# The output projection of a cross-attention tile, moved behind the first two groups of transposes of the next tile

## The chip, the cores and the metric

One core of a Trainium2 chip runs the whole program: four transformer layers, each a cross-attention and a mixture of experts. The metric is the device time of one launch in microseconds. Engine names are those of the profile: PE (TensorE matmuls), PEld (its weight loads), DVE (VectorE), ACT (ScalarE), POOL (GpSimd), SP (SyncE).

## The reference, cut to what matters

The change touches three of the four cross-attentions: those of layers 0, 2 and 3 (L0, L2, L3). Each adds to the residual `x` (4 batches of 512 tokens, width 128) an attention over 77 context rows:

```python
qh = heads(layernorm(x) @ Wq + bq);  kh = heads(ctx @ Wk + bk);  vh = heads(ctx @ Wv + bv)
score = einsum('bhqd,bhkd->bhqk', qh, kh) / sqrt(D)      # L2: + mask * -1e9, L3: barred keys at -inf
attn = softmax(score, axis=-1)
out = einsum('bhqk,bhkd->bhqd', attn, vh)
x = x + merge_heads(out) @ Wo + bo
```

L0 and L2 have 16 heads of 8, L3 has 8 heads of 64 and no biases. The cross-attention of layer 1 is another function and is not touched.

## The kernel before

`cross_attention` cuts the 2048 tokens into 16 tiles of 128. Every engine has its own program, written out by hand as a Python loop over tiles; within an engine the instructions run in the order in which they are written, and semaphores tie the engines together.

For a tile n, PE's function `tile(n)` does this:

- `turn(n, g)`: four transposes of the probabilities of one group of four heads into a PSUM bank (line 529). It waits for `normed`, which POOL's `divide` (line 441) raises twice for a tile, once for each half of the heads. L0 and L2 have four groups, L3 two.
- ACT's `group_turned` (line 635) copies each turned group to `probT`.
- `product(n, g)`: probabilities by values (line 540 in L0 and L2, 542 in L3). It waits for that copy.
- `scores(n + 3)`: queries by keys for the tile three ahead (lines 95 to 97 in L0 and L2, where each product is split in three; line 518 in L3). In L0 and L2 it stands ahead of the products of groups 2 and 3, in L3 behind all products. It waits until DVE has read the scores of the tile before it.
- ACT's `mixed(n)` (line 639) copies the summed products from PSUM to `mixedT`.
- `output(n)` (line 550): `mixedT` by the output weights, one product in L0 and L2, four in L3. It waits for `mixed(n)` and stands at the end of the tile. DVE's `add(n)` (line 745) adds its result to the residual.
- In tiles 0, 4 and 8 `next_queries` (line 483) also projects the queries of the next batch; ACT copies them (lines 621 and 627). In L0 and L2 that projection goes to the same PSUM bank as the products.

DVE's tile n: `shift(n + 2)` (a maximum over the scores, line 728, and a subtraction, line 729; for unmasked scores of L2 and for L3 first an addition of the mask), `add(n - 1)`, `add_up(n + 1)` (sums and reciprocals of both halves, lines 737 and 738). In tiles 0, 3 and 6 it also lays out the keys of a further batch (`spread_keys`, line 688). ACT's tile n has, between copies, the exponential of tile n + 2 (line 631). Behind the last tile PE transposes two batches for the next stage (`nxt.norm.turn`, line 284), which ACT copies (line 291); then all engines meet at a barrier.

Of the kernel before, what the change touches and what calls it, by code (L numbers as in the profile page):

```python
# [27 lines left out]
TILES = BATCH * SEQ // P  # L28
# [288 lines left out]
def cross_attention(c, norm, fetch, nxt, tag, H, D, score_scale, mask):  # L317
# [26 lines left out]
    with ExitStack() as ctx:  # L344
# [51 lines left out]
        def later(n, k):  # L396
            return 0 <= n + k < TILES

        with nc.Block() as block:
# [68 lines left out]
            def _(pe):  # L468
# [10 lines left out]
                def queries(b, j):  # L479

                    if j >= 2:
                        pe.wait_ge(q_ready, b * FB + j - 1)
                    pe.matmul(ps[:, Q[j % 2], :], wq[:, j * P:(j + 1) * P], c.normT[:, b * SEQ:(b + 1) * SEQ], start=True, stop=True).then_inc(q_done, 1)

                def wait_scores_read(n):
                    if mask is None or masked_on_pe(n):
                        pe.wait_ge(shifted, n + 1)
                    else:
                        pe.wait_ge(masked, masks_added(n) + 1)
# [32 lines left out]
                def turn(n, g):  # L522

                    pe.wait_ge(normed, n * 2 + g * 2 // GROUPS + 1)
                    if g >= 2:
                        pe.wait_ge(turn_read, n * GROUPS + g - 1)
                    for a in range(GROUP):
                        h = g * GROUP + a
                        last = pe.transpose(ps[0:KEYS, TURN + g % 2, a * P:(a + 1) * P], prob[:, n % PROBS, h * KEYS:(h + 1) * KEYS], c.ident[:])  # L529
                    last.then_inc(turned, 1)  # L530

                def product(n, g):

                    if n == 0 and g == 0 and biased:
                        pe.wait_ge(v_ready, GROUP)
                    pe.wait_ge(turn_read, n * GROUPS + g + 1)
                    for a in range(GROUP):
                        h = g * GROUP + a
                        if FB == 1:
                            last = pe.matmul(ps[a * COLS:(a + 1) * COLS, PV, 0:P], v_all[:, n // TPB, h, :], probT[:, h, :], start=(g == 0), stop=(g == GROUPS - 1))  # L540
                        else:
                            last = pe.matmul(ps[h % 2 * D:(h % 2 + 1) * D, PV, h // 2 * P:(h // 2 + 1) * P], v_all[:, n // TPB, h, :], probT[:, h, :], start=True, stop=True)
                    if g == GROUPS - 1:
                        last.then_inc(pv_done, 1)

                def output(n):
                    pe.wait_ge(mixed_ready, n + 1)
                    pe.wait_ge(y_added, n + 1)
                    for j in range(FB):
                        last = pe.matmul(ps[:, Y, 0:P], mixedT[:, j * P:(j + 1) * P], wo[:, j, :], start=(j == 0), stop=(j == FB - 1))  # L550
                    last.then_inc(y_done, 1)

                def tile(n):
                    project = list(range(FB)) if n % TPB == 0 and later(n, TPB) else []

                    def next_queries():
                        if project:
                            queries(n // TPB + 1, project.pop(0))

                    next_queries()  # L560
                    turn(n, 0)
                    next_queries()
                    turn(n, 1)
                    next_queries()
                    for g in range(GROUPS):
                        if g > 0 and g + 1 < GROUPS:
                            turn(n, g + 1)
                        if g == SCORES_AT and later(n, AHEAD):
                            scores(n + AHEAD)
                        product(n, g)  # L570
                        next_queries()
                    if SCORES_AT == GROUPS and later(n, AHEAD):
                        scores(n + AHEAD)
                    output(n)

                if not biased:
                    pe.wait_ge(v_ready, BATCH)
# [15 lines left out]
                for n in range(TILES):  # L593
                    tile(n)
                wait_scores_read(TILES - 1)
                nxt.norm.turn(pe, 0, 0)
                nxt.norm.turn(pe, 1, 1)

            @block.scalar
# [1944 lines left out]
```

## Time and profile before

| | us |
|---|---|
| median of 3 runs | 1961.55 |
| lowest and highest run | 1961.02, 1966.17 |
| span of the profiled execution | 1960.8 |
| tiles of L0, L2 and L3 in it (first product to the barrier) | about 102, 109 and 83 |
| PE busy, share of the span | 93% |
| mean granted TensorE clock | 0.974 |

The span runs from the first to the last instruction. No time of its own is listed for the profiled execution; its span is 0.2 below the fastest run and 0.75 below the median.

### The profile page before, as it was taken

What the parts mean: (1) busy time and instruction counts of PE and PEld (TensorE: products, weight loads), DVE (VectorE), ACT (ScalarE), POOL (GpSimd) and SP (SyncE); (2) the same over time, 40 slices, a digit from 0 to 9 for tenths busy, and PEclk for the clock granted to TensorE, in tenths of its full rate; (3) what the DMA queues carried; (4) which work ended last, traced back from release to release, by engine and by line L of the source; (5) the groups of instructions that cost most, each with busy time, mean ns of one, the idle gap of its engine ahead of it and who ended that gap; (6) DMA issues with size and microseconds to landing.
All of it is one profiled execution on the core that took longest, in us unless ns stands there. A gap on an engine that the chain in (4) does not pass through costs nothing. (4 is left out here: it accounts for less than half of the span.)

```text
span 1960.8 us, 29985 instructions
## 1 busy us (share of the span) xinstructions
PE 1818.4 (93%) x11163; PEld 1272.5 (65%) x11163; DVE 1500.0 (77%) x2712; ACT 1015.9 (52%) x1506; POOL 829.8 (42%) x667
## 2 busy tenths in 40 slices
PE   5888999789999999999989999889899999989898
PEld 4667888544544444445447777677567789967676
DVE  6878986766777676767758888888699965567798
ACT  3656888356666766666644555455400130045686
POOL 3633221266767676767661344365301402012231
PEclk9999999789999999999998999999999999999899
DMA  1001111100000000000000212000000110000032
GB/s 66 2 12 58 65 65 54 52 1 1 1 1 1 1 1 1 1 1 1 1 4 17 87 65 86 13 1 2 17 11 27 32 54 1 0 13 1 22 115 97
DMA packets 21195, 51.52 MB, mean 26 GB/s; under 512 B 3563, under 2 KB 11383, under 8 KB 18116
## 3 DMA queue, kind: packets, MB, share of 16 engines
q1 hardware_dynamic: 20596, 49.53, 7.4%
q8 instruction: 83, 1.36, 0.3%
q14 instruction: 52, 0.43, 0.1%
q10 hardware_dynamic: 464, 0.20, 0.1%
HBM read 48.48 MB, written 1.25 MB: 25 GB/s over the span
## 5 line engine op out<-in xcount | busy, mean ns | idle before, releaser
L1605 POOL TENSOR_TENSOR sb_L_total<-sb_L_total,sb_L_probT 128x512 f32<-128x512 f32 (+1 forms) x192 | 268.7, 1424 | 59.5 <-ACT sb_L_probT L1911 56.6
L441 POOL TENSOR_TENSOR sb_L_prob<-sb_L_prob,sb_L_rsum 128x616 f32<-128x616 f32 (+1 forms) x96 | 105.7, 1123 | 239.6 <-DVE sb_L_rsum L738 239.6
L1911 ACT ACTIVATE sb_L_probT<-banks 128x1024 f32<-128x1024 f32 x128 | 131.3, 1025 | 113.4 <-PE banks L1738 113.2
L1968 DVE TENSOR_REDUCE sb_L_top_tok<-banks 128x2 f32<-128x1024 f32 x128 | 155.7, 1217 | 6.1 <-PE banks L1705 4.3
L1748 PE MATMUL banks<-sb_L_probT,sb_L_v 128*64 128x512 f32 x512 | 137.1, 615 | 0.2 <-DVE sb_L_mixedT L2019 0.2
L2335 DVE SCALAR_TENSOR_TENSOR sb_L2f_hid<-banks,sb_L2f_weight,sb_L2f_hid 128x512 f32<-128x512 f32 x176 | 123.2, 748 | 2.6 <-PE banks L97 1.6
L1602 POOL TENSOR_TENSOR sb_L_total<-sb_L_probT 128x512 f32<-128x512 f32 x64 | 80.7, 1282 | 104.5 <-ACT sb_L_probT L1911 104.5
L2405 DVE SCALAR_TENSOR_TENSOR sb_resid<-banks,sb_L2f_weight,sb_resid 128x128 f32<-128x128 f32 x192 | 67.2, 351 | 60.9 <-PE banks L97 56.3
L1310 DVE TENSOR_TENSOR sb_L0f_hid_low<-sb_L0f_raw,sb_L0f_hid_high 128x1024 fp32r<-128x1024 f32 x64 | 88.3, 1396 | 28.8 <-ACT sb_L0f_hid_high L1266 28.4
L635 ACT ACTIVATE sb_L_probT<-banks 77x512 f32<-77x512 f32 x160 | 86.7, 586 | 41.5 <-PE banks L529 41.5
L1247 ACT ACTIVATE sb_L1f_gate<-banks 112x512 f32<-112x512 f32 x96 | 57.6, 600 | 93.2 <-PE banks L97 93.2
L1986 DVE TENSOR_TENSOR sb_L_q_sq_low<-sb_L_q_sq,sb_L_q_sq_high 128x512 fp32r<-128x512 f32 x32 | 25.4, 793 | 102.1 <-ACT sb_L_q_sq_high L1863 102.1
L1255 ACT ACTIVATE sb_L0f_raw<-banks,sb_L0f_b 128x512 f32<-128x512 f32 x128 | 86.6, 681 | 26.2 <-PE banks L97 26.0
L529 PE MATMUL banks<-sb_ident,sb_L_prob 128*77 128x128 f32 x640 | 92.9, 279 | 0.0
L1303 DVE TENSOR_TENSOR sb_L1f_raw<-sb_L1f_gate,banks 112x512 f32<-112x512 f32 x96 | 65.8, 686 | 35.4 <-PE banks L97 31.9
L263 ACT ACTIVATE sb_norm_root<-sb_norm_square 128x8 f32<-128x8 f32 (+4 forms) x16 | 3.4, 210 | 171.6 <-DVE sb_norm_square L257 147.6
L95 PE MATMUL banks<-sb_L2f_w_high,sb_L2f_hidT_low 128*128 128x384 f32 x256 | 85.6, 334 | 1.7 <-DVEq L2397 1.7
L97 PE MATMUL banks<-sb_L2f_w_high,sb_L2f_hidT_high 128*128 128x384 f32 x256 | 85.5, 334 | 0.0
L96 PE MATMUL banks<-sb_L2f_w_low,sb_L2f_hidT_high 128*128 128x384 f32 x256 | 85.5, 334 | 0.0
L95 PE MATMUL banks<-sb_L2f_w_high,sb_norm_low 128*128 128x512 f32 x192 | 80.8, 421 | 5.0 <-DVE sb_L2f_hid L2335 4.9
L1310 DVE TENSOR_TENSOR sb_L1f_hid_low<-sb_L1f_raw,sb_L1f_hid_high 112x512 fp32r<-112x512 f32 x96 | 85.0, 886 | 0.1
L529 PEld LDWEIGHTS banks<-sb_ident,sb_L_prob 128*77 128x77 f32 x640 | 72.1, 147 | 19.7 <-issue 18.9
(432 smaller groups left out, 5410.4 us busy)
## 6 DMA issues: line engine op xcount, KB each, us to landing
sb_L0f_wide<-spread_L0f SPq DMA_DIRECT2D x7, 1024.0 KB, 6.7
sb_L1f_wide<-spread_L1f SPq DMA_DIRECT2D x7, 1024.0 KB, 7.2
sb_L3f_wide<-spread_L3f SPq DMA_DIRECT2D x7, 1024.0 KB, 4.9
sb_fetched<-L2f_w SPq DMA_DIRECT2D x12, 256.0 KB, 2.6
sb_fetched<-L1f_gu SPq DMA_DIRECT2D x8, 336.0 KB, 3.1
sb_fetched<-L0f_w SPq DMA_DIRECT2D x8, 259.0 KB, 2.9
sb_fetched<-L0f_w SPq DMA_DIRECT2D x8, 256.0 KB, 3.1
sb_normT<-L2f_w SPq DMA_DIRECT2D x2, 768.0 KB, 4.2
```

Of the source, the lines that this page charges most:

```text
L95: pe.matmul(out, sl, mh, start=start, stop=False)
L96: pe.matmul(out, sh, ml, start=False, stop=False)
L441: pool.tensor_tensor(grid, grid, bcast(rsum[:, n % PROBS, half], [None, KEYS]), ALU.mult).then_inc(normed, 1)
L529: last = pe.transpose(ps[0:KEYS, TURN + g % 2, a * P:(a + 1) * P], prob[:, n % PROBS, h * KEYS:(h + 1) * KEYS], c.ident[:])
L635: act.activation(probT[:, g * GROUP:(g + 1) * GROUP, :].rearrange("k h t -> k (h t)"), ps[0:KEYS, TURN + g % 2, :], ACT.Copy).then_inc(tur ...
L1255: act.activation(raw[:, s % lag, f, :], ps[:, n % HBANKS, :], func, bias=bias).then_inc(hid_read, 1)
L1310: dve.tensor_tensor(hid_low[:, s % SLOTS, at, :], raw[:, s % lag, at, :], hid_high[:, s % SLOTS, at, :], ALU.subtract).then_inc(hid_ready, 1)
L1605: pool.tensor_tensor(sums[rows], sums[rows], probT[rows, k, h], ALU.add).then_inc(added[h], 1)
L1748: last = pe.matmul(O[HEAD[h]], v[:, turn % 2, k, HEAD[h]], probT[:, k, h, :], start=(k == 0), stop=False)
L1911: act.activation(probT[:, k], ps[:, slot:slot + 2, :], ACT.Exp).then_inc(exped, 1)
L1968: dve.tensor_reduce(top_tok[:, :, k:k + 1].rearrange("p h k -> p (h k)"), ps[:, banks:banks + 2, :], AX.X, ALU.max).then_inc(bound_read, 1)
L2335: ins = dve.scalar_tensor_tensor(out=hid[:, n, :], in0=ps[:, n % BANKS, :], scalar=share, in1=hid[:, n, :], op0=ALU.mult, op1=ALU.add)
```

## The change

`output(n)` leaves the end of tile n. It is issued in tile n + 1, behind that tile's `turn(n + 1, 0)` and `turn(n + 1, 1)` and ahead of its first `product`. In L0 and L2, in the tiles with a projection of queries (4 and 8), it stands at the tile's start instead, where it stood before, since the projection writes the bank that `mixed` reads. The last output goes between the two `nxt.norm.turn` of the stage's end. No instruction is added or dropped, and the programs of the other engines are the same.

```diff
+                    early = split and project and n > 0
+                    if early:
+                        output(n - 1)
                     next_queries()
                     turn(n, 0)
                     next_queries()
                     turn(n, 1)
                     next_queries()
+                    if n > 0 and not early:
+                        output(n - 1)
                     for g in range(GROUPS):
...
                     if SCORES_AT == GROUPS and later(n, AHEAD):
                         scores(n + AHEAD)
-                    output(n)
...
                 wait_scores_read(TILES - 1)
                 nxt.norm.turn(pe, 0, 0)
+                output(TILES - 1)
                 nxt.norm.turn(pe, 1, 1)
```

PE in L0, from the last two products of tile 0 into tile 1. L540 is `product`, L529 `turn`, L550 `output`. Before:

```order
L540 MATMUL banks<-sb_L_probT,sb_L_v_all 32x128 x8
L550 MATMUL banks<-sb_fetched,sb_L_mixedT 128x128
L529 MATMUL banks<-sb_ident,sb_L_prob 77x128 x8
L540 MATMUL banks<-sb_L_probT,sb_L_v_all 32x128 x4
L529 MATMUL banks<-sb_ident,sb_L_prob 77x128 x4
```

And with the change:

```order
L540 MATMUL banks<-sb_L_probT,sb_L_v_all 32x128 x8
L529 MATMUL banks<-sb_ident,sb_L_prob 77x128 x8
L550 MATMUL banks<-sb_fetched,sb_L_mixedT 128x128
L540 MATMUL banks<-sb_L_probT,sb_L_v_all 32x128 x4
L529 MATMUL banks<-sb_ident,sb_L_prob 77x128 x4
```

The output and the eight transposes have changed places; L2 reads the same.

PE in L3, tile 1 to tile 2. L542 is `product`, L518 `scores`. Before:

```order
L550 MATMUL banks<-sb_fetched,sb_L_mixedT 128x128 x4
L529 MATMUL banks<-sb_ident,sb_L_prob 77x128 x8
L542 MATMUL banks<-sb_L_probT,sb_L_v_all 64x128 x8
L518 MATMUL banks<-sb_L_kdiag,sb_L_qT 128x154 x4
L550 MATMUL banks<-sb_fetched,sb_L_mixedT 128x128 x4
```

And with the change:

```order
L529 MATMUL banks<-sb_ident,sb_L_prob 77x128 x8
L550 MATMUL banks<-sb_fetched,sb_L_mixedT 128x128 x4
L542 MATMUL banks<-sb_L_probT,sb_L_v_all 64x128 x8
L518 MATMUL banks<-sb_L_kdiag,sb_L_qT 128x154 x4
L529 MATMUL banks<-sb_ident,sb_L_prob 77x128 x8
```

Here `scores` already stood between the products and the output; now the transposes stand there too.

PE at the end of L3; L284 is `nxt.norm.turn`. Before:

```order
L542 MATMUL banks<-sb_L_probT,sb_L_v_all 64x128 x8
L550 MATMUL banks<-sb_fetched,sb_L_mixedT 128x128 x4
L529 MATMUL banks<-sb_ident,sb_L_prob 77x128 x8
L542 MATMUL banks<-sb_L_probT,sb_L_v_all 64x128 x8
L550 MATMUL banks<-sb_fetched,sb_L_mixedT 128x128 x4
L284 MATMUL banks<-sb_ident,sb_norm_stage 128x128 x8
```

And with the change:

```order
L542 MATMUL banks<-sb_L_probT,sb_L_v_all 64x128 x8
L529 MATMUL banks<-sb_ident,sb_L_prob 77x128 x8
L550 MATMUL banks<-sb_fetched,sb_L_mixedT 128x128 x4
L542 MATMUL banks<-sb_L_probT,sb_L_v_all 64x128 x8
L284 MATMUL banks<-sb_ident,sb_norm_stage 128x128 x4
L550 MATMUL banks<-sb_fetched,sb_L_mixedT 128x128 x4
L284 MATMUL banks<-sb_ident,sb_norm_stage 128x128 x4
```

The output of tile 14 stands behind the transposes of tile 15, and that of tile 15 between the two transposed batches.

## Rows read from the trace of the kernel before

**Rows 1.** Windows: stretch, length, busy of PE, PEld, DVE, ACT, POOL; clock, DMA.

```profile
41.00:143.00 102.00, 89.07 (x973) 66.68 (x971) 80.92 (x138) 60.35 (x104) 50.05 (x36) 1.00 0.01 1
1293.00:1402.00 109.00, 96.66 (x1027) 74.28 (x1026) 92.02 (x143) 60.02 (x104) 54.53 (x42) 1.00 0.01 1
1748.00:1831.00 83.00, 77.17 (x651) 60.97 (x649) 63.43 (x159) 45.35 (x79) 20.61 (x30) 0.99 0.00 1
...
160.00:170.00 10.00, 5.32 (x22) 4.36 (x22) 9.82 (x55) 2.13 (x2) 4.68 (x3) 0.66 0.01 2
```

**Rows 2.** Groups by line on PE in L0 (L2's read the same), and L3.

```profile
L540 PE MATMUL banks<-sb_L_probT,sb_L_v_all 77*32 77x128 f32 x512 | 24.6, 282 | 5.8 <-ACT sb_L_probT L635 5.7
L550 PE MATMUL banks<-sb_fetched,sb_L_mixedT 128*128 128x128 f32 x32 | 7.8, 326 | 6.4 <-ACT sb_L_mixedT L639 6.4
...
L550 PE MATMUL banks<-sb_fetched,sb_L_mixedT 128*128 128x128 f32 x128 | 17.2, 277 | 2.1 <-ACT sb_L_mixedT L639 2.1
```

**Rows 3.** Timeline of L0, tile 5 into 6: start, length, instruction, idle before.

```profile
79.45 0.65 PE L540 MATMUL banks<-sb_L_probT,sb_L_v_all 77*32 77x128 f32 x16
...
80.16 0.28 ACT L639 ACTIVATE sb_L_mixedT<-banks 128x128 f32<-128x128 f32 x1 [1.70 <-PE banks L540]
80.49 0.49 PE L550 MATMUL banks<-sb_fetched,sb_L_mixedT 128*128 128x128 f32 x2 [0.40 <-ACT sb_L_mixedT L639]
80.81 1.04 PE L529 MATMUL banks<-sb_ident,sb_L_prob 128*77 128x128 f32 x8
...
81.45 1.08 ACT L635 ACTIVATE sb_L_probT<-banks 77x512 f32<-77x512 f32 x2 [1.01 <-PE banks L529]
82.10 0.43 PE L540 MATMUL banks<-sb_L_probT,sb_L_v_all 77*32 77x128 f32 x8 [0.25 <-ACT sb_L_probT L635]
...
82.45 0.66 PE L529 MATMUL banks<-sb_ident,sb_L_prob 128*77 128x128 f32 x4
...
83.05 0.43 PE L540 MATMUL banks<-sb_L_probT,sb_L_v_all 77*32 77x128 f32 x8
```

**Rows 4.** Timeline of L0, tile 0 into tile 1: ACT's extra copy of queries.

```profile
48.09 0.62 ACT L627 ACTIVATE sb_L_q_high<-sb_L_qT 128x512 fp32r<-128x512 f32 x1
...
49.85 0.43 PE L540 MATMUL banks<-sb_L_probT,sb_L_v_all 77*32 77x128 f32 x8 [0.25 <-ACT sb_L_probT L635]
```

**Rows 5.** Timeline of L0, tiles 6 and 7: DVE's key layout and what follows it.

```profile
83.69 3.59 POOL L441 TENSOR_TENSOR sb_L_prob<-sb_L_prob,sb_L_rsum 128x616 f32<-128x616 f32 x2 [1.61 <-DVE sb_L_rsum L738]
...
84.42 1.78 DVE L688 TENSOR_TENSOR sb_L_kdiag<-sb_L_kT_high,sb_head 128x1232 fp32r<-128x1232 f32 x1
...
86.13 1.43 DVE L728 TENSOR_REDUCE sb_L_top<-banks 128x16 f32<-128x1232 f32 x1
...
87.59 1.44 DVE L729 TENSOR_TENSOR sb_L_prob<-banks,sb_L_top 128x1232 f32<-128x1232 f32 x1
...
90.06 0.39 PE L95 MATMUL banks<-sb_L_kdiag,sb_L_q_low 128*128 128x308 f32 x1
```

**Rows 6.** Timeline of L3, tile 1 into tile 2, and DVE's next start.

```profile
1760.41 1.05 PE L550 MATMUL banks<-sb_fetched,sb_L_mixedT 128*128 128x128 f32 x8
1760.61 0.80 DVE L723 TENSOR_TENSOR sb_L_prob<-banks,sb_L_barred 128x616 f32<-128x616 f32 x1 [0.57 <-PE banks L518]
1761.30 1.04 PE L529 MATMUL banks<-sb_ident,sb_L_prob 128*77 128x128 f32 x8
...
1762.58 1.14 PE L542 MATMUL banks<-sb_L_probT,sb_L_v_all 77*64 77x128 f32 x16 [0.25 <-ACT sb_L_probT L635]
...
1763.95 1.36 POOL L441 TENSOR_TENSOR sb_L_prob<-sb_L_prob,sb_L_rsum 128x308 f32<-128x308 f32 x2 [3.04 <-DVE sb_L_rsum L738]
...
1765.01 0.80 DVE L723 TENSOR_TENSOR sb_L_prob<-banks,sb_L_barred 128x616 f32<-128x616 f32 x1 [0.57 <-PE banks L518]
```

**Rows 7.** Timeline of L3, tile 15: POOL's divisions and PE's products.

```profile
1824.11 1.36 POOL L441 TENSOR_TENSOR sb_L_prob<-sb_L_prob,sb_L_rsum 128x308 f32<-128x308 f32 x2 [3.54 <-DVE sb_L_rsum L738]
...
1826.20 1.32 PE L542 MATMUL banks<-sb_L_probT,sb_L_v_all 77*64 77x128 f32 x16
```

## The prediction

> **What bounds the kernel now.** I read the windows over the three stages first. In L0 PE is busy 89 of 102 us, DVE 81, ACT 60, POOL 50; in L2 it is 97 and 92 of 109, in L3 77 and 63 of 83, with the TensorE clock granted at 1.00, 1.00 and 0.99 [rows 1]. PE is the busiest in all three, with DVE close behind in L2. The stages lie one behind the other with a barrier between, so what PE saves in one is saved at the end, unless another engine takes over.
>
> Then the groups by line, to see where PE waits. In L0 it is idle 6.4 us in front of the output projection, always for ACT's copy `mixed`, and 5.8 us in front of the products, for the copy of the turned group; L2's rows read the same. In L3 the output costs only 2.1 us of idle time, since the scores stand between. A group's last columns are its idle time before and who ended it [rows 2]. 6.4 us over 16 tiles is 0.40 a tile.
>
> Last the timeline of one tile boundary. PE's last products start at 79.45, ACT copies from 80.16 to 80.44, and PE, which waited 0.40, starts the output at 80.49. Eight transposes follow at 80.81, and then PE waits 0.25 for ACT's copy of the first group before the product at 82.10 [rows 3]. The reader is to see two waits in series, each with work beside it that does not depend on it: the transposes don't need `mixed`, and the output doesn't need the turned group. The change crosses them.
>
> **The change, step by step, L0.** From the last products to the next tile's first product PE now takes 82.10 - 79.45 = 2.65 us. Packed without a wait, the same instructions take: the 16 product records 0.65 less their overlap with what follows (0.43 less 0.35 from 82.10 to 82.45, so 0.08), 0.57; the transposes 1.04 less their overlap (0.66 less 0.60 from 82.45 to 83.05), 0.98; the output 0.32, from 80.49 to 80.81 [rows 3]. Together 1.87, so a boundary gains 0.78. The idle times alone give 0.40 + 0.25 = 0.65. These are the two bounds; I take the middle, 0.72. The profile's matmul ends are modelled, which is why the two differ.
>
> The Trainium skill says the same of its source: in Perfetto Trace Analysis, section Tensor Engine Instruction, the end reported for a matmul is an estimate. By that rule starts are the better ruler, and a boundary would gain 0.78 rather than 0.65; this case's rows show both figures and do not decide.
>
> Is ACT in time? With transposes right behind the products, the copy `mixed` (0.28) runs during them, and the copy of the first group starts 0.64 behind their start (80.81 to 81.45), as now. Packed transposes and output take 0.98 + 0.32 = 1.30, and the product starts 1.29 behind the transposes already today [rows 3], so the copy is ready just when PE is.
>
> Counting the boundaries of L0. Those into tiles 4 and 8 keep the old order: 0. Those into tiles 2, 3, 6, 7, 10, 11, 12 and 14 gain 0.72 each: 5.8. Into tiles 1, 5 and 9 ACT has the high part of the queries (0.62, from 48.09) between `mixed` and the first group's copy; that copy would then run from 48.71 and take 0.54 (half of 1.08, [rows 3]), so the product can start at about 49.3 instead of 49.85 [rows 4]. With the lower bound 0.35 I take 0.45 each: 1.35. Into tiles 13 and 15 I count 0, as no scores are left to issue and PE there hangs on the exponential of tile 15 and, through ACT, on the square roots for the next stage. At the end the last `mixed` is covered by the first transposed batch: 0.40 as at any output. Sum 7.5.
>
> What is late next is DVE. It works without a pause from the scores of tile 8 through the key layout (84.42, 1.78 us) to the end of the subtraction at 87.59 + 1.44 = 89.03, and PE starts the next scores, which need it, at 90.06 [rows 5]: a slack of 1.03, less 0.05 for a handover (80.44 to 80.49, [rows 3]). Two boundaries lie between, which take away 2 x 0.72 = 1.44, so PE would wait about 0.5 there. POOL's division beside it ends at 87.28 [rows 5], near enough to its transposes for another 0.1. So L0 gains 7.5 - 0.6 = 6.9. Bounds: no stall, 7.5; twice the stall, 6.3. Tile 4 has the queries as cover, and tile 1 comes too early to have lost its slack.
>
> **L2** has the same order. DVE has one more pass of 1.44 us (the size of line 729's in [rows 5]) in every second tile, and PE more matmuls in the others, as its busier rows show [rows 1]. The lag behind the key layouts is thus longer, and the first one may show too: I charge 0.7 more, between 0 and twice it. L2: 7.5 - 0.6 - 0.7 = 6.2.
>
> **L3.** Output, transposes and wait take 1762.58 - 1760.41 = 2.17; packed 0.89 + 0.98 = 1.87. PE alone would go from 4.40 a tile (1760.61 to 1765.01) to 4.10 [rows 6]. But the transposes now come 0.9 sooner, and POOL's second half is not ready: from DVE's start at 1760.61 to POOL's end at 1765.31 are 4.70. From there on a handover (0.05), the second four transposes (half of 0.98), the output (0.89), and products and scores to DVE's start (1762.58 to 1765.01, 2.43) make 8.56 for two tiles, or 4.28 each [rows 6]. So a tile gains 0.12, and eleven or twelve of them 1.3. At the tail the output of tile 14, which filled PE's wait for POOL, now stands behind it: POOL ends at 1825.47, then half the transposes and 0.89 of output bring the last products to 1826.9 instead of 1826.20 [rows 7]: 0.7 lost. The output's wait in the last tile, a third of 2.1 us [rows 2], is covered: 0.7 back, less 0.3 as the second batch is now behind the output. L3 gains 1.0, between -0.7 and 3.
>
> DMAs, weights and the other stages are as before: the moved instructions issue none. DVE's `add(n)` comes later by up to 1 us, yet DVE gets to it only after `shift`, 2.9 us behind the scores.
>
> Sum: 6.9 + 6.2 + 1.0 = 14.1. Against the median of 1961.55, which is 0.75 above the span in which this was worked out, that gives **1947.5**.
>
> **The rivals.** Below 0.3% (5.9 us) a measurement of this kernel can't tell a change from none.
>
> *As forecast*: faster by 9 to 19.5 us, 0.68.
>
> *The chain of DVE, ACT and POOL takes over* wherever PE gets ahead: scores, shift, exponential, copy, product. For it: DVE is busy 92 of 109 us in L2, so 6.2 saved leaves it 90% busy. Against it: in L0 there are 21 us in which DVE does nothing [rows 1], more than the change uses. Then L0 and L2 would keep half of their 13.1, some 6.5, and L3 nothing: 1955.0, 1953 to 1956, faster if barely: 0.14.
>
> *No stall and full packing*: 8 x 0.78 + 3 x 0.55 + 0.5 = 8.4 in L0 and L2 each, 3 in L3, 20 in all: 1941.8; from 19.5 on, 0.06.
>
> *The clock.* Behind L0 there are ten us with PE busy 5.3 and a granted clock of 0.66, so between its two levels of 1.2 and 2.4 GHz; 3.4 us of clock time [rows 1]. All later stages begin earlier and may meet the fall elsewhere. Three more such stretches would take 10 of the 14, which ends within 0.3%, at 1957.7: 0.08. The clock of L0 and L2 itself is at full, and a denser PE gives it no reason to fall.
>
> The Trainium skill (TensorE: Matmul & The Clock Gate, section What's actually happening) says that the window of the clock gate runs free of the kernel's start. By that rule this is scatter from run to run, not a loss of the change, which agrees with one run of three at 1966.17; it would leave the median near 1947.5.
>
> *Slower*: DVE waits for the later output. `add(n - 1)` stands ahead of `add_up(n + 1)`, and all that POOL and the transposes get hangs on that. If a tile's transposes were late by more than `shift` lasts (86.13 to 89.03, 2.9 us, [rows 5]), the output, `add`, the sums, the division and the next transposes would close a ring that PE can't get ahead of. It decides where PE would wait over 1.5 us a tile for POOL at its first transposes, since PE's part between them and DVE's `add` is 1.3 us; then, at half a us lost in each of some 40 tiles, the time is 1961.5 + 20 = 1981, and 1969 if only L0 and L2's first halves do it. No row of L0 shows PE waiting for POOL: 0.04.
>
> The chances: faster 0.68 + 0.14 + 0.06 = 0.88, less 0.01 for the chain case's edge, 0.87; same 0.09; slower 0.04. The range goes from 1942.0, nearly all packed, to 1955.0, into the second rival. It leaves out some 0.04 below and 0.14 above.
>
> **What the next profile would show.** Right: line 550's idle time on PE falls from 6.4 to about 1 in L0 and in L2 (tiles 3 and 7 remain), and the boundary of 2.65 to 1.9; L0 and L2 take some 95 and 103 us from their first product. A new wait of about half a us stands before line 95 behind the key layout of tile 6. In L3 every second tile waits 0.1 to 0.2 for POOL before its second transposes, and the period is 4.3. Wrong: a repeated wait of ACT, DVE or POOL of 0.3 or more in each tile of L0, or a lower clock in the stages behind.

## The result, and the profile after

The changed kernel takes 1954.41 us, the median of four runs (1949.63 to 1956.5), beside 1963.17 for the kernel before in the same comparison (four runs, 1961.02 to 1966.17): a ratio of 0.9945, 95% interval 0.9922 to 0.9967. A second comparison (told below, as the changed kernel again) gave 0.9953, 0.9937 to 0.9968; it leaves out one run of the kernel before, of 2518.87 us at a granted clock of 0.649, as a slow one. So by the two ratios the change is worth 10.8 and 9.2 us, where 14.1 were forecast. The intervals are 6.5 to 15.3 us, which still holds the forecast, and 6.3 to 12.4, which does not. The kernel is faster by more than the 0.3% that was set as the bound (the weak ends, 0.33 and 0.32%, only just), and the median lies inside the range, 0.6 below its upper end.

The profiled execution of the changed kernel took 1949.63 us with a span of 1947.9 and a granted clock of 0.976. From here on a stage's length runs from its first product (line 540 or 542) to POOL's first instruction behind its barrier, since this tells the stage apart from the clock of all the others:

| stage length, us | before | after |
|---|---|---|
| L0 | 43.60 to 143.80 = 100.20 | 43.37 to 137.43 = 94.06 |
| L2 | 1295.33 to 1403.55 = 108.22 | 1288.71 to 1392.30 = 103.59 |
| L3 | 1752.62 to 1831.78 = 79.16 | 1740.08 to 1819.53 = 79.45 |
| sum | 287.58 | 277.10 |

L0 gave 6.1 and L2 4.6, and L3 lost 0.3: 10.5 us. First the windows over the three stages after, which answer to [rows 1], and short ones near the end of L0, L2 and L3: stretch, length, busy time of PE, PEld, DVE, ACT and POOL, granted clock.

```profile
41.00:137.00 96.00, 89.42 (x972) 67.73 (x970) 80.94 (x138) 60.55 (x104) 50.01 (x36) 0.98 0.01 1
1286.00:1392.00 106.00, 98.32 (x1030) 75.69 (x1028) 92.21 (x143) 60.44 (x104) 54.50 (x42) 0.98 0.01 1
1738.00:1819.00 81.00, 76.60 (x642) 61.63 (x641) 62.60 (x158) 45.13 (x78) 20.57 (x30) 0.98 0.00 1
...
127.00:129.00 2.00, 0.73 (x10) 0.47 (x11) 1.17 (x4) 1.44 (x3) 1.58 (x2) 0.94 0.00 0
129.00:131.00 2.00, 2.00 (x10) 1.80 (x9) 1.31 (x6) 1.47 (x4) 0.81 (x1) 0.50 0.00 0
...
1378.00:1380.00 2.00, 2.00 (x10) 1.98 (x10) 1.96 (x12) 0.98 (x3) 0.89 (x1) 0.51 0.00 0
...
1810.00:1812.00 2.00, 0.98 (x6) 0.76 (x7) 1.12 (x5) 1.75 (x4) 1.36 (x2) 0.88 0.00 0
1812.00:1814.00 2.00, 2.00 (x11) 2.00 (x11) 1.97 (x8) 0.94 (x2) 0.00 (x0) 0.50 0.00 0
```

The clock column has changed: 1.00, 1.00 and 0.99 before, 0.98 in all three now. The short windows show where: near the end of the stage it is at 0.50, its lower level of 1.2 GHz. From here on such a stretch is called a fall of the clock, and the last tiles of a stage its tail. Before, the last 14 us of L0 (129 to 143) read 1.00 in one window. PE's busy time misleads here: it is 2.00 of 2.00 us with only 10 records, because each takes twice as long.

Next the groups by line on PE, two of L0 and two of L3, answering to [rows 2]: busy time, mean ns of one, idle time before and who ended it.

```profile
L540 PE MATMUL banks<-sb_L_probT,sb_L_v_all 77*32 77x128 f32 x512 | 24.9, 285 | 3.5 <-ACT sb_L_probT L640 2.8
L550 PE MATMUL banks<-sb_fetched,sb_L_mixedT 128*128 128x128 f32 x32 | 6.7, 293 | 0.8 <-ACT sb_L_mixedT L644 0.8
...
L529 PE MATMUL banks<-sb_ident,sb_L_prob 128*77 128x128 f32 x124 | 18.8, 285 | 3.3 <-POOL sb_L_prob L441 3.0
L550 PE MATMUL banks<-sb_fetched,sb_L_mixedT 128*128 128x128 f32 x128 | 17.9, 285 | 0.1
```

The output's idle time in L0 went from 6.4 to 0.8 us, and that of the products from 5.8 to 3.5, as the two crossed waits should. In L3 the 2.1 us of the output went to 0.1, and in their place the transposes wait 3.3 us, nearly all for POOL: 1.33 of it before those of tile 14 and 1.65 before those of tile 15.

Last the timeline of the changed kernel. The rows are the boundary into tile 1, tile 6 into 7, an undisturbed boundary of L0, the transposes of tile 15 of L0, the products of L2's tile 13, the transposes of L3's tiles 2 and 3, and those of its tile 15. All but those of tile 15 of L0 and of L2 answer to rows of before: [rows 4], [rows 5], [rows 3], [rows 6] and [rows 7].

```profile
49.02 0.43 PE L540 MATMUL banks<-sb_L_probT,sb_L_v_all 77*32 77x128 f32 x8
...
81.52 1.78 DVE L693 TENSOR_TENSOR sb_L_kdiag<-sb_L_kT_high,sb_head 128x1232 fp32r<-128x1232 f32 x1
...
84.43 0.43 PEld L529 LDWEIGHTS banks<-sb_ident,sb_L_prob 128*77 128x77 f32 x4 [0.30 <-POOL sb_L_prob L441]
...
86.18 0.19 PEld L95 LDWEIGHTS banks<-sb_L_kdiag,sb_L_q_low 128*128 128x128 f32 x1 [0.38 <-DVE sb_L_prob L734]
...
112.10 0.64 PE L540 MATMUL banks<-sb_L_probT,sb_L_v_all 77*32 77x128 f32 x16
112.68 1.10 PE L529 MATMUL banks<-sb_ident,sb_L_prob 128*77 128x128 f32 x8
112.81 0.28 ACT L644 ACTIVATE sb_L_mixedT<-banks 128x128 f32<-128x128 f32 x1 [0.98 <-PE banks L540]
113.38 1.08 ACT L640 ACTIVATE sb_L_probT<-banks 77x512 f32<-77x512 f32 x2 [0.29 <-PE banks L529]
113.61 0.39 PE L550 MATMUL banks<-sb_fetched,sb_L_mixedT 128*128 128x128 f32 x2
114.02 0.43 PE L540 MATMUL banks<-sb_L_probT,sb_L_v_all 77*32 77x128 f32 x8
...
128.69 1.97 PE L529 MATMUL banks<-sb_ident,sb_L_prob 128*77 128x128 f32 x8 [0.98 <-POOL sb_L_prob L441]
...
1377.08 0.91 PE L540 MATMUL banks<-sb_L_probT,sb_L_v_all 77*32 77x128 f32 x16 [0.94 <-ACT sb_L_probT L640]
...
1747.76 1.32 PE L529 MATMUL banks<-sb_ident,sb_L_prob 128*77 128x128 f32 x8
...
1752.08 1.03 PE L529 MATMUL banks<-sb_ident,sb_L_prob 128*77 128x128 f32 x8
...
1811.02 1.79 PE L529 MATMUL banks<-sb_ident,sb_L_prob 128*77 128x128 f32 x8 [1.65 <-POOL sb_L_prob L441]
```

The boundary takes 114.02 - 112.10 = 1.92 us instead of 2.65, and no PE row in it waits. Before the transposes of tile 15 PE stands idle for 0.98 us, and for 1.65 in L3, where before it had the output to do; right behind it eight transposes take 1.97 instead of 1.10. In L2 the fall came earlier, at 1378.0, and not behind tile 15's wait: it stands behind a wait of 0.94 for ACT in tile 13. That wait is new too. The profile before has none of more than 0.40 there; L0 and L2 have it in all ten profiles in which the outputs of the tiles ahead of it stand behind or between transposes.

### The profile page after: what moved, and what is told of

Same layout as the page of the kernel before. It is cut to its first block and busy times, and to the rows that moved or that the text cites. A ratio compares the mean times of both kernels' runs of the same rounds, so it can differ in the third digit from the quotient of the medians.

```text
span 1947.9 us, 29985 instructions
## 1 busy us (share of the span) xinstructions
PE 1814.5 (93%) x11163; PEld 1271.6 (65%) x11163; DVE 1501.5 (77%) x2712; ACT 1015.5 (52%) x1506; POOL 833.9 (43%) x667
## 5 line engine op out<-in xcount | busy, mean ns | idle before, releaser
L529 PE MATMUL banks<-sb_ident,sb_L_prob 128*77 128x128 f32 x640 | 98.8, 288 | 4.8 <-POOL sb_L_prob L441 4.4
L529 PEld LDWEIGHTS banks<-sb_ident,sb_L_prob 128*77 128x77 f32 x640 | 72.8, 151 | 32.6 <-issue 21.3
```

## The experiments

**The theory to test.** The crossing works as forecast; what is missing was lost in the tails of the stages, where PE's wait for POOL, which nothing covers (an open wait), brings its clock down. Its rivals: the falls came by chance and have nothing to do with the order; or the stages gain less because DVE or POOL hold them. Each experiment is the changed kernel with one more edit, unless it says otherwise. `moved(n)` tells whether the output of tile n stands in tile n + 1; where not, it stands at the end of tile n as before.

**The tail as before.**

```diff
+                def moved(n):
+                    return n < TILES - 2
...
+                    if not moved(n):
+                        output(n)
```

> The changed kernel, but the outputs of tiles 14 and 15 stand at the end of their own tiles, as before the change. Stage times run from the stage's first product (line 540 or 542) to POOL's first instruction behind it; in the changed kernel L0 takes 94.06 us, L2 103.59, L3 79.45. Theory A (the change costs at the tail: PE has nothing left for its wait for POOL's division, the output stands behind that wait, and the TensorE clock falls to 0.50 there because PE stands idle): the wait before the transposes of tile 15 is filled, the clock stays at 1.00, and L0 takes 92.9, L2 102.4, L3 77.5, together 4.3 us less. Rival B (the fall of the clock came by chance, the tail has no part in it): L0 94.1, L2 103.6, L3 79.0 or more, and a fall shows in the tails again in at least one of the three. Rival C (tail neither costs nor gives): within 0.3 us of the changed kernel in each.

Measured: L0 93.16, L2 102.60, L3 77.86, together 3.5 us less than the changed kernel's first profile; the ratio to the kernel before, 0.9942 (0.9924 to 0.9960), doesn't show it. The clock stays at 1.00 in all three tails. Here is L3's, as windows and as PE's timeline:

```profile
1810.00:1812.00 2.00, 1.98 (x18) 1.52 (x18) 1.16 (x6) 1.73 (x4) 1.02 (x2) 1.00 0.00 0
1812.00:1814.00 2.00, 1.30 (x18) 0.82 (x15) 1.55 (x7) 0.96 (x2) 0.00 (x0) 1.00 0.00 0
```

```profile
1809.45 1.16 PE L550 MATMUL banks<-sb_fetched,sb_L_mixedT 128*128 128x128 f32 x8 [0.70 <-ACT sb_L_mixedT L650]
1810.44 1.29 PE L529 MATMUL banks<-sb_ident,sb_L_prob 128*77 128x128 f32 x8
```

The output fills PE's wait for POOL again. But this edit moves work as well as clock, so it does not yet tell the two apart.

**The tail filled with work that nobody needs.**

```diff
+                    if n == TILES - 1:
+                        keep_busy(pe, c, TURN, 6 if split else 10)
                     turn(n, 0)
```

> The changed kernel plus matmuls into a free bank, whose result nobody reads, right before the transposes of tile 15 in each stage (6 in L0 and L2, 10 in L3, about 0.13 us each). They do no work, so only the clock can gain. Theory A (PE's idle time before those transposes brings the clock down): the granted clock stays at 1.00 through the tails, L0 92.8, L2 102.6, L3 78.0. Rival B (chance, or something else than idle PE): the clock falls to 0.50 as in the changed kernel, and L0 94.1, L2 103.6, L3 79.5, or a little more where the filling ends late.

Measured: L0 92.87, L2 102.42, L3 78.27; ratio 0.9916 (0.9897 to 0.9934). Windows of L0's tail, and PE's timeline there:

```profile
127.00:129.00 2.00, 1.67 (x25) 1.21 (x22) 1.51 (x4) 1.44 (x3) 1.24 (x2) 1.00 0.00 0
129.00:131.00 2.00, 1.98 (x24) 1.65 (x22) 0.96 (x4) 1.86 (x4) 1.15 (x1) 1.00 0.00 0
```

```profile
127.98 1.61 PE L103 MATMUL banks<-sb_ident 128*128 128x128 f32 x12
129.43 1.04 PE L529 MATMUL banks<-sb_ident,sb_L_prob 128*77 128x128 f32 x8
```

With more instructions all three stages are shorter, by 1.2 us each, close to the theory's numbers. No work was taken away, so such a gain can only come from the clock: the windows lie where the changed kernel's read 0.94 and 0.50. But it takes a profile of the changed kernel without a fall to say what the filling itself does, and two things in it are chance. L2's fall in the first profile began at 1378.0, in tile 13, where this filling does not reach. And in a later profile of the changed kernel (below) L0 and L2 had no fall without any filling, and took 92.67 and 102.12. With the clock up the filling costs 0.2 to 0.3. The row at 127.98 shows why: the six matmuls are 12 records and take 1.61 us, where the expectation reckoned with 0.13 each.

**The key layout in a tile that has cover.**

```diff
-                    if n in (0, 3, 6):
-                        spread_keys(n // 3 + 1)
+                    if n in (0, 4, 8):
+                        spread_keys(n // 4 + 1)
```

(and POOL's `low_keys` of L0 and L2 likewise, in tiles 4 and 8 instead of 3 and 6)

> The changed kernel, but the key layouts for tiles 8 and 12 are made in tiles 4 and 8 (DVE's and POOL's), where PE has the query projections of about 1 us more, instead of in tiles 3 and 6. Theory A (the layout behind tile 6 makes PE wait, which the forecast charged with 0.6 in L0 and 1.3 in L2): L0 takes 93.4 and L2 102.4, and the waits before line 95 and before the transposes of tile 7 (0.38 and 0.30 in L0) are gone. Rival B (DVE and POOL are late in tiles 4 and 8 as well, and the wait only moves): L0 94.1, L2 103.6, with a new wait before the scores in tile 5 or 9. Rival C (in L2 the lag comes from DVE being full, not from the layout): L0 93.4, L2 within 0.3 of 103.6.

Measured: L0 93.49, L2 101.34, L3 80.51; ratio 0.9919 (0.9901 to 0.9937). In L0 the wait before line 95 and the one before the transposes of tile 7's third group are gone. PE's timeline there, and a row of L2:

```profile
84.67 0.66 PE L529 MATMUL banks<-sb_ident,sb_L_prob 128*77 128x128 f32 x4
...
86.03 0.39 PE L95 MATMUL banks<-sb_L_kdiag,sb_L_q_low 128*128 128x308 f32 x1
...
1327.91 1.10 PE L529 MATMUL banks<-sb_ident,sb_L_prob 128*77 128x128 f32 x8 [1.05 <-POOL sb_L_prob L441]
```

L0's tail has a fall of the clock like the changed kernel's, so the 0.57 between them is what the late layouts give; 0.6 was charged for the stall. L2 had no fall this time, so it is to be held against the changed kernel's undisturbed L2 (102.12, below): 0.78. That is a balance and not the layouts' price, for in L2 rival B is half right. The stall behind tile 6 is gone, and a new wait of 1.05 for POOL stands before the transposes of tile 5, behind the layout in tile 4. The expectation looked for it before the scores. L3 is longer by 1.1 because its fall lasted longer, which nobody had expected:

```profile
1818.00:1822.00 4.00, 4.00 (x28) 3.45 (x28) 1.94 (x8) 1.17 (x3) 0.00 (x0) 0.53 0.00 0
1822.00:1826.00 4.00, 3.08 (x15) 2.63 (x13) 0.29 (x1) 1.30 (x3) 0.00 (x0) 0.61 0.00 0
```

**The output between the two first groups' transposes.**

```diff
                     turn(n, 0)
                     next_queries()
-                    turn(n, 1)
-                    next_queries()
                     if n > 0 and not early:
                         output(n - 1)
+                    turn(n, 1)
+                    next_queries()
```

> The changed kernel, but the output projection of tile n - 1 stands between the two first groups' transposes of tile n. Theory A: in L0 and L2 both waits are still covered (ACT's copy of the mixed values by the first four transposes, its copy of the turned group by the output and the second four), so L0 and L2 stay within 0.3 us of 94.06 and 103.59; in L3 the output fills PE's wait for POOL's second half, the period falls from 4.31 us a tile to about 4.15, and L3 takes 76 to 78 instead of 79.45. Rival B (POOL sets L3's pace whatever stands where): L3 stays at 79.5. Rival C (four transposes are too short a cover for the copy of the mixed values): a wait of 0.2 to 0.3 returns before line 550 in each tile and L0 takes 97 to 98.

Measured: L0 94.02, L2 102.16, L3 80.62; ratio 0.9949 (0.9931 to 0.9966). L0 is as expected: four transposes cover the copy of the mixed values. L2 only looks 1.4 better: it had no fall. For L3 both theories missed. PE's timeline, a tile of L3:

```profile
1794.82 0.61 PE L550 MATMUL banks<-sb_fetched,sb_L_mixedT 128*128 128x128 f32 x4
1795.26 0.60 PE L529 MATMUL banks<-sb_ident,sb_L_prob 128*77 128x128 f32 x4
1795.79 1.41 PE L542 MATMUL banks<-sb_L_probT,sb_L_v_all 77*64 77x128 f32 x16
...
1800.15 1.41 PE L542 MATMUL banks<-sb_L_probT,sb_L_v_all 77*64 77x128 f32 x16
```

POOL no longer holds the transposes, but the second group's now stand right before the products, and the products take 1.41 instead of 1.09: their second half waits inside the row for ACT's copy of that group. 1800.15 - 1795.79 = 4.36 a tile, against 4.31 on average in the changed kernel and 4.40 before. Whichever way the two are ordered, one handover stays open.

**Both edits together.** `moved` as in the first, the key layouts as in the third.

> The two edits of the runs before together: outputs of tiles 14 and 15 at the end of their own tiles, and the key layouts for tiles 8 and 12 made in tiles 4 and 8. Theory A (the two costs are separate): L0 takes 93.16 - 0.57 = 92.6 us, L2 101.3, L3 77.9, and no fall of the clock in the three tails; 5.3 us less than the changed kernel, so a ratio to the kernel before of about 0.992. Rival B (the late layouts already gave PE the time that the tail gives, one and the same slack): no better than either alone, L0 93.2, L2 101.3 to 102.6, L3 77.9.

Measured: L0 93.73, L2 102.95, L3 77.65; ratio 0.9939 (0.9926 to 0.9953). L0 and L2 are no better than with one edit alone, as rival B says, but the trace has another reason for it: a fall in each of their tails, though the outputs of tiles 14 and 15 stand in their old places. PE's timeline and the windows in L0:

```profile
128.17 0.49 PE L550 MATMUL banks<-sb_fetched,sb_L_mixedT 128*128 128x128 f32 x2 [0.40 <-ACT sb_L_mixedT L650]
128.75 1.86 PE L529 MATMUL banks<-sb_ident,sb_L_prob 128*77 128x128 f32 x8
```

```profile
127.00:129.00 2.00, 1.19 (x16) 0.71 (x13) 1.23 (x4) 1.44 (x3) 1.52 (x2) 0.98 0.00 0
129.00:131.00 2.00, 2.00 (x16) 1.43 (x14) 1.24 (x5) 1.60 (x4) 0.87 (x1) 0.50 0.00 0
```

The output fills only a part: waits of 0.33 and 0.40 remain ahead of the fall, and PE is busy 1.19 of 2 us. So the theory was too neat: a fall also comes behind a wait that is half filled.

**Only the tail moved.** The kernel before, with `moved(n)` true for tiles 14 and 15 alone.

> The kernel before, in which only the outputs of tiles 14 and 15 are moved (behind the first two groups' transposes of tile 15, and between the transposes for the next stage). Theory A (PE's uncovered idle time in the tail brings the clock down, whatever the other tiles do): the clock falls behind the transposes of tile 15 in at least two of the three stages, and each such stage takes 0.7 to 2 us more than before: L0 101 to 102 (before 100.2), L2 109 to 110 (before 108.2), L3 80 to 81 (before 79.2). Rival B (the fall needs the denser tiles of the changed kernel): no fall, and L0 100.2, L2 108.2, L3 79.5.

Measured: L0 99.65, L2 108.91, L3 79.23, one time of 1959.62. Only L2 had a fall. Theory A, which wanted two, missed; so did rival B, which wanted none. The run is also a weaker test than was meant: in L0 and L2 the transposes of tile 15 wait only 0.24 for POOL here, and 0.84 and 0.85 stand before the products behind them; L2's fall begins 2.7 us after that. In L3 the wait before the transposes was open, 1.75, and the clock held. L0 shows what the tail's move gives while the clock holds: 0.55, most of it as the last output's wait is covered.

**The output behind the scores.**

```diff
-                    if n > 0 and not early:
+                    held = split and n > 0 and not early
+                    if n > 0 and not early and not held:
                         output(n - 1)
+                    if held:
+                        pe.wait_ge(mixed_ready, n)
...
                             scores(n + AHEAD)
+                        if held and g == SCORES_AT:
+                            output(n - 1)
```

> The changed kernel, but in L0 and L2 the output projection of tile n - 1 stands behind the scores of tile n, about 3.3 us later; L3 is as in the changed kernel. This drives the slower rival of the forecast over its edge. Theory A (DVE's add waits for the output and holds the sums, POOL's division and the next transposes): in L0 DVE reaches its add 1.0 us behind the output now, so it is held about 2.3 us, POOL's first half has 0.7 of slack before the next transposes, and PE loses some 1.6 us or more in each tile: L0 110 or more instead of 94.06, L2 the like, with PE waiting for POOL before line 529. Rival B (DVE has idle time enough to take the delay): L0 within 1 us of 94, no such wait.

Measured: one time of 2040.08, L0 132.94. The slower rival is real. The timeline of one tile:

```profile
119.54 0.38 PE L550 MATMUL banks<-sb_fetched,sb_L_mixedT 128*128 128x128 f32 x2
120.03 0.29 DVE L755 TENSOR_TENSOR sb_resid<-banks,sb_resid 128x128 f32<-128x128 f32 x1 [3.11 <-PE banks L550]
121.33 2.39 POOL L441 TENSOR_TENSOR sb_L_prob<-sb_L_prob,sb_L_rsum 128x616 f32<-128x616 f32 x2 [4.60 <-DVE sb_L_rsum L748]
122.60 1.23 PE L529 MATMUL banks<-sb_ident,sb_L_prob 128*77 128x128 f32 x8 [2.11 <-POOL sb_L_prob L441]
```

One ring in four rows: DVE's `add` waited 3.11 for the output, POOL for DVE's sums, PE's next transposes 2.11 for POOL. The clock fell too, to 0.83 over the whole stage.

**The changed kernel again**, beside these.

> The changed kernel once more, beside the others on the same chip. Theory A (the order of instructions alone sets the stages; the clock falls in unfilled tails only): L0, L2 and L3 take 92.4 to 94.1, 102.2 to 103.6 and 78 to 80.6, and a fall shows in the tail of at least two of the three; ratio to the kernel before 0.993 to 0.996. Rival B (the falls of the first profile were chance): no fall in the tails, ratio 0.992 or less.

Measured: L0 92.67, L2 102.12, L3 79.56; ratio 0.9953 (0.9937 to 0.9968). L0 and L3 lie in theory A's ranges and L2 just below its own; the falls are between the two, as only L3 had one. L0 and L2 without a fall are 1.4 and 1.5 shorter than in the first profile, by the same instructions. PE's timeline and the windows of L0's tail:

```profile
128.97 1.10 PE L529 MATMUL banks<-sb_ident,sb_L_prob 128*77 128x128 f32 x8 [0.97 <-POOL sb_L_prob L441]
```

```profile
127.00:129.00 2.00, 0.70 (x17) 0.19 (x9) 1.45 (x4) 1.44 (x3) 1.30 (x2) 1.00 0.00 0
129.00:131.00 2.00, 1.88 (x20) 1.50 (x21) 1.02 (x5) 1.83 (x4) 1.09 (x1) 1.00 0.00 0
```

The wait is the same, 0.97 against 0.98, and the clock holds.

**The best of each stage together.** In L0 and L2 the changed order with the six unread matmuls, in L3 the tail as before, and the late key layouts.

> What did best in each stage so far, together: in L0 and L2 the changed order with the six unread matmuls before the transposes of tile 15, in L3 the outputs of tiles 14 and 15 at the end of their own tiles, and the key layouts for tiles 8 and 12 in tiles 4 and 8 everywhere. Theory A (the layout's stall and the uncovered tail are separate, and the clock stays up in the tails): L0 92.3 us, L2 101.6, L3 77.7, or 5.5 less than the changed kernel's 277.1 in sum; beside the kernel before a ratio of 0.991 to 0.993, since the falls of the clock in the unchanged stages, 45 to 58 us of lost clock time in all, move any run by some us. Rival B (the clock falls in a tail as it did with the outputs left in place): the stage with a fall takes 1.4 more, 93.7 or 103.0.

Measured: L0 92.41, L2 101.61, L3 77.65, and the clock at 1.00 through all three tails; sum 271.67, 5.4 less than the changed kernel's first profile. All three lengths came within some 0.1 us of theory A. The ratio is 0.994 (0.9921 to 0.9959), which can't be told from the changed kernel's. The stretches that no edit touches are a likely reason: from L0's end to L2's first product the profiles took 1150.5 to 1158.0 us (and 1162.8 once, with the output behind two products), 1154.1 in this one and 1151.3 in the changed kernel's first. It beats the kernel before; that it beats the changed one is shown by the stages and not by the time.

**The output behind two products.** As behind the scores, but `if held and g == 1: output(n - 1)` behind `product(n, g)`.

> The changed kernel, but in L0 and L2 the output projection of tile n - 1 stands behind the second group's products of tile n, about 1.8 us later; L3 is as in the changed kernel. It looks for the point from which the slower rival decides, between the changed kernel (L0 94.1) and the output behind the scores (L0 132.9). Theory A (worked out from DVE's and POOL's slack: DVE reaches its add 1.0 us behind the output, POOL's first half is ready 0.66 before the transposes that need it): DVE is held about 0.7 us a tile, which POOL's slack takes in; L0 92.5 to 96, and PE waits for POOL 0 to 0.2 a tile. Rival B (the edge lies where the forecast put it, at 2.9 us): L0 92.7 to 94.1 and no wait for POOL. Rival C (any wait of DVE comes back on PE in full): 0.7 a tile, L0 100 or more.

Measured: one time of 1983.19, L0 102.36. The timeline of one tile:

```profile
119.52 0.29 DVE L755 TENSOR_TENSOR sb_resid<-banks,sb_resid 128x128 f32<-128x128 f32 x1 [0.82 <-PE banks L550]
...
122.11 1.10 PE L529 MATMUL banks<-sb_ident,sb_L_prob 128*77 128x128 f32 x8
123.55 0.42 PE L540 MATMUL banks<-sb_L_probT,sb_L_v_all 77*32 77x128 f32 x8 [0.34 <-ACT sb_L_probT L645]
```

DVE waits 0.82 for the output, and POOL's slack takes it in: the transposes do not wait. Rival B's edge of 2.9 falls, as DVE is held already here. The tile is 0.34 longer for the other half of the crossing: nothing covers ACT's copy of the first group. Some 12 tiles make 4 us of that; most of the rest is two falls of the clock, the second of which lasted to the end of the stage, so the length missed the theory's 96 at most.

**The count of falls**, with two profiles more.

> The changed kernel a third time, for the count of tails with a fall of the clock: so far 9 of 15 tails in which the wait before the transposes of tile 15 stands open, 2 of 10 with the outputs in their old places there, 0 of 5 with the unread matmuls. Theory A (an open wait makes a fall likely, when it comes is chance): one to three of the three tails. Rival B (the tails differ by chance alone, 11 of 30): about one of the three, and as many in the filled kernel beside it. Without a fall L0 takes 92.7 us, L2 102.1, L3 78.3; a fall adds 1.3 to 1.5.

Measured: L0 96.22, L2 102.13, L3 80.78, a fall in L0 and L3. L0's lasted from 128.6 to the stage's end and cost 3.5 us.

> The changed kernel with the unread matmuls before the transposes of tile 15, once more. Theory A: no fall in any of the three tails, L0 92.9, L2 102.4, L3 78.3. Rival B: a fall in one of them, that stage 1.3 us longer.

Measured: L0 94.33, L2 102.39, L3 78.27. L0 has a fall after all, but it begins at 123.2, behind the wait of 0.94 in tile 13, which the filling does not reach; the fall in L2 of the changed kernel's first profile began behind the same wait (the count in the expectation above had taken it in). So the falls are counted by what they stand behind, without the two kernels whose output stands behind products or scores:

| PE's wait | falls behind it |
|---|---|
| for POOL before the transposes of tile 15, open (0.97 to 1.75 us) | 9 of 15: L0 4 of 5, L2 0 of 4, L3 5 of 6 |
| outputs of tiles 14 and 15 in their old places | 2 of 10 |
| filled with unread matmuls | 0 of 8 |
| 0.94 for ACT in tile 13, L0 and L2 | 2 of 20 |

L0 and L2 of the run in which only the tail was moved, with their wait in two pieces, had one fall in two. The same wait of 0.97 or 0.98 was followed by a fall in L0 four times in five and in L2 never, and nothing here says why.

## Why the forecast was nearly right, and where it wasn't

**The crossing.** Forecast 0.72 a boundary, between 0.65 and 0.78; measured 1.92 instead of 2.65, so 0.73. The middle was right. Neither ruler of the prediction was: packed it would be 1.87, and ACT's copy of the first group (half of the 1.08 from 113.38) ends at 113.92, about when PE is ready.

**L0.** Forecast 6.9, measured with the clock up 100.20 - 92.67 = 7.5. Into tile 1 the first product starts at 49.02, not 49.85; less the 0.23 by which the stage began earlier that is 0.60, where 0.45 was taken, three times. The end gives some 0.5, not 0.40. The stall behind the key layout of tile 6 came where it was forecast, 0.38 before line 95 and 0.30 before the transposes, and cost 0.63, where 0.6 was charged. Here is what each boundary gained: the time from a tile's first product to the next tile's, before less after, and under "end" the rest of the stage. L0 and L2 are from the changed kernel again, which had no fall there, and L3 from the tail as before.

| into tile | 1 | 2 | 3 | 4 | 5 | 6 | 7 | 8 | 9 | 10 | 11 | 12 | 13 | 14 | 15 | end |
|---|---|---|---|---|---|---|---|---|---|---|---|---|---|---|---|---|
| L0 | 0.61 | 0.74 | 0.73 | 0.00 | 0.60 | 0.73 | 0.73 | -0.63 | 0.61 | 0.73 | 0.72 | 0.74 | 0.73 | 0.00 | 0.00 | 0.49 |
| L2 | 0.63 | 0.44 | 0.75 | -0.01 | 0.24 | 0.72 | 0.30 | -1.06 | 0.63 | 0.75 | 0.73 | 0.73 | 0.75 | 0.00 | 0.00 | 0.49 |
| L3 | 0.32 | -0.17 | 0.36 | 0.05 | 0.32 | -0.17 | 0.29 | -0.07 | 0.31 | -0.18 | 0.36 | -0.17 | 0.36 | -0.45 | 0.14 | 0.00 |

In L0 eight boundaries gained in full, as forecast. But the one into tile 13 is among them, where nothing was forecast, and the one into tile 14 is not: there the new wait of 0.94 takes the gain.

**L2.** Forecast 6.2, measured with the clock up 108.22 - 102.12 = 6.1, and this is luck: two errors cancel. Away from the layouts the boundaries gain what they do in L0; the row's full values, three of 0.63, eight of 0.74 and 0.49, would make 8.3, where 7.5 were forecast. The boundaries into tiles 2, 5, 7 and 8 fall short of that by 0.30, 0.39, 0.44 and 1.06: 2.2, where 1.3 was charged. The shortfalls into 7 and 8 are the price of the layout in tile 6, since they go when it is moved. Those into 2 and 5 stand behind the layouts of tiles 0 and 3, and with the second of these moved to tile 4 the shortfall into 5 grew by another 0.65. That the one into 2 is a layout's too is read off its place and not tested.

**L3.** Forecast 1.0, made of 1.3 for the tiles and 0.3 lost at the end. With the tail as before the stage is 79.16 - 77.86 = 1.3 shorter, and with the filled tail 79.16 - 78.27 = 0.9. POOL's second half holds every second tile as described: the transposes at 1747.76 and 1752.08 take 1.32 and 1.03, the periods are 4.57 and 4.04, and 4.31 on average, where 4.28 was forecast. The sum is in part luck. The eight plain tiles gained 0.68, under 0.09 each instead of 0.12; the boundaries into tiles 1, 5 and 9, which the prediction gave no term of their own, gained 0.95; and tiles 13 and 14, shorter than 4.40 before, lost 0.3.

**The step that failed.** These add up to 7.5 + 6.1 + 0.9 = 14.5, beside a forecast of 14.1. The sentence that was wrong is in the rival on the clock: "The clock of L0 and L2 itself is at full, and a denser PE gives it no reason to fall". The stages as a whole are denser, but their tails are not. At tile 15 PE is bound by POOL, and in L0 and L2 at tile 13 by ACT. The prediction saw this in L3, priced it as 0.7 of work behind a wait, and counted L0's and L2's tails as 0, without asking what else an open wait of 1 to 1.6 us does. Over its three profiles the changed kernel's L0 averages 94.3, L2 102.6 and L3 79.9, which is 1.7, 0.5 and 1.7 above their lengths at full clock (92.67, 102.12, and 78.27 of the filled tail): 3.8 of the 14.5, leaving 10.7. L2's part stands behind tile 13's wait and the others behind tile 15's. The two timed comparisons gave 10.8 and 9.2 (0.0055 and 0.0047 of 1963). The agreement is rough: three profiles are few, each comparison is uncertain by some 3 or 4 us, and the kernel before has one profile, without a fall, so what falls cost it on average is not known. That 1954.41 is still in the range is close to luck, at 0.6 from its end; 1.6 of the 6.9 above the forecast come from the kernel before, whose median here is 1963.17 and not 1961.55.

What is shown: a fall makes a stage longer by more than a us with the same instructions, and behind tile 15's wait it came in 9 of 15 tails where the wait was open and in 0 of 8 where it was filled. What isn't settled is when an open wait is followed by a fall; the same wait of 0.97 or 0.98 was in one execution and not in another. The Trainium skill (TensorE: Matmul & The Clock Gate, section What's actually happening) has the gate's window run free of the kernel's start. By that rule it is a matter of phase, which agrees with L0 of the changed kernel, where the clock fell in two of three profiles; but L3 had a fall in all three, and L2 in none behind tile 15's wait, so chance alone is not shown to be all of it. The prediction cited this rule and drew from it that the median would not suffer. That was the wrong half: a loss whose moment is chance still has a mean.

**The rivals.** The chain of DVE, ACT and POOL did not take over: no repeated wait of 0.3 or more stands in L0's tiles. No stall and full packing did not happen either. The slower rival's mechanism is real, but its edge was put at 2.9 us of lateness. DVE reaches its `add` only 1.0 us behind the output, and POOL's slack takes in about as much again: at 1.8 us later DVE waits 0.82 and PE doesn't, at some 3.3 later PE waits 2.11 a tile.

## What to carry to other kernels

When two engines hand work back and forth twice in series, put the work that each wait doesn't depend on in front of it; here the gain was a little over the sum of both waits per boundary (0.73 and 0.65), and it holds as long as no third engine's slack is used up. Then look at the ends of the stage on their own: an instruction that leaves the place in which it filled another engine's wait opens that wait, and on PE an open wait can cost its clock besides. Try the last iterations in their old order, or filled, and compare single stages in the traces, and more than one profile of each, since the total can hide 5 us of gain in three stages behind what nobody touched. And where a forecast comes true, check its terms one by one: L2's came true by two errors of 0.8 and 0.9 that cancel.

## What the runs showed of the hardware

PE's clock fell to 0.50, which is 1.2 GHz, behind single idle times of only 0.94 to 1.66 us, and three times behind smaller ones in a row (0.33 and 0.40 twice, 0.84 and 0.33 once). A fall cost a stage 1.2 to 1.5 us, 2.5 in L3 of the changed kernel's third profile, and 3.5 where it lasted to the end of L0. It made eight transposes take 1.79 to 1.99 us instead of 1.04 to 1.10. Six matmuls whose result nobody reads, 12 records of 1.61 us together, put into a wait of some 1 us, made L0 longer by 0.2 with the clock up, where a fall makes it longer by 1.4. And the unchanged 1150 us between L0 and L2 differed by up to 12.3 us from one profile to another, and by 7.5 without the profile of the output behind two products.
